# A transformer layer with sixteen heads and top-2 experts: values projected by token rows, moved between partitions and scaled on GpSimd

## The reference

```python
z = _layernorm(patches, ln1_g, ln1_b); z = einsum('bnp,pe->bne', z, W_proj) + b_proj; z = _layernorm(z, ln2_g, ln2_b)
h = concatenate([cls, z]) + pos_emb; h = concatenate([h, txt], axis=1)          # (32, 69, 256)
q, k, v = (einsum('bsd,hpd->bhsp', _layernorm(h), w) + b for each of q, k, v)
attn = softmax(einsum('bhqp,bhkp->bhqk', q, k) / 8, axis=2)                       # over the queries
h = h + einsum('bhqk,bhkp->bqhp', attn, v).reshape(..., 1024) @ l_w.T + l_b
h = h + moe(_layernorm(h))        # top 2 of 8 experts, capacity 690, 256 -> 1024 -> gelu -> 256
```

## Time and profile before

| what | value |
|---|---|
| median of 3 runs | 701.25 us (701.14 to 701.62) |
| the profiled execution: its time, and the span of its profile | 702.5 us, 700.7 us |
| TensorE busy | 682.9 us, 97% |
| VectorE busy | 505.5 us, 72% |
| ScalarE busy | 294.9 us, 42% |
| GpSimd busy | 277.6 us, 40% |
| share of TensorE in the chain that ended last | 73%, VectorE 14% |

### The profile page before, as it was taken

The page is one execution under the profiler, slowest core; times in us unless marked ns, Lnnn a source line. Parts: engine busy times, 40 slices in busy tenths (PEclk is TensorE's granted clock), DMA queues, the critical chain, the costliest instruction groups (busy, mean ns, idle before and its releaser), DMA issues.

```text
span 700.7 us, 16956 instructions
## 1 busy us (share of the span) xinstructions
PE 682.9 (97%) x6671; PEld 649.4 (93%) x6671; DVE 505.5 (72%) x1159; ACT 294.9 (42%) x652; POOL 277.6 (40%) x294
## 2 busy tenths in 40 slices
PE   8999999999999999999999989999999999999995
PEld 6878899999999999999999988999999999999995
DVE  6978876988979889798877756765656484737471
ACT  4454545445454454544544215343424251615130
POOL 4664010130401304011030452766666666665715
PEclk9999999999999999999999999999999999999998
DMA  7931000000000000000000413445454444434203
GB/s 257 271 95 29 2 1 18 12 16 11 19 17 11 17 11 19 18 10 17 12 19 18 138 43 91 121 83 137 69 133 85 112 89 101 103 84 102 24 8 30
DMA packets 51579, 42.99 MB, mean 61 GB/s; under 512 B 25493, under 2 KB 45139, under 8 KB 51515
## 3 DMA queue, kind: packets, MB, share of 16 engines
q1 hardware_dynamic: 20171, 27.85, 12.8%
q0 software_dynamic: 29168, 11.61, 10.5%
q10 hardware_dynamic: 2176, 2.64, 1.3%
HBM read 32.76 MB, written 10.25 MB: 61 GB/s over the span
## 4 chain that ended last, share of the span: by engine, by line
PE 73%; DVE 14%; issue 4%; DMA 3%; SPq 2%; POOL 2%; ACT 1%; POOLq 0%; DVEq 0%; ACTq 0%
PE pair L1518 11%; PE pair L1520 11%; PE pair L1519 11%; PE lone L1518 9%; PE lone L1519 8%; PE lone L1520 8%; PE pair L1636 4%; PE ct_ps L1646 4%; PE vt_ps L1623 3%; DVE vals L1126 2%; DVE zsum L1116 2%; DVE top L1107 2%; SPq L437 2%; DMA raw<-w_qkv 1%; DVE expo L1110 1%
## 5 line engine op out<-in xcount | busy, mean ns | idle before, releaser
L781 POOL DMA_INDIRECT out<-yrow,held x48 | 100.9, 2101 | 62.8 <-DVE yrow L1479 46.3
L1002 ACT ACTIVATE act_f<-pair 128x348 f32<-128x348 f32 (+1 forms) x120 | 49.0, 457 | 92.0 <-PE pair L1520 88.9
L762 POOL DMA_INDIRECT held<-token_rows,found_ix x48 | 70.3, 1464 | 33.5 <-issue 22.0
L1518 PE MATMUL pair<-xe_hi,fc_hi 128*128 128x348 f32 (+1 forms) x256 | 82.1, 321 | 0.6 <-DVE xe_lo L1449 0.3
L1520 PE MATMUL pair<-xe_hi,fc_lo 128*128 128x348 f32 (+1 forms) x256 | 82.2, 321 | 0.0
L1519 PE MATMUL pair<-xe_lo,fc_hi 128*128 128x348 f32 (+1 forms) x256 | 82.1, 321 | 0.0
L1518 PE MATMUL lone<-pj_hi,act_hi 128*116 128x256 f32 (+1 forms) x256 | 72.2, 282 | 0.0
L1520 PE MATMUL lone<-pj_hi,act_lo 128*116 128x256 f32 (+1 forms) x256 | 71.9, 281 | 0.0
L1519 PE MATMUL lone<-pj_lo,act_hi 128*116 128x256 f32 (+1 forms) x256 | 71.8, 280 | 0.0
L845 ACT ACTIVATE expo<-expo 69x552 f32<-69x552 f32 x64 | 42.5, 664 | 55.5 <-DVE expo L1110 54.8
L831 ACT ACTIVATE qkv<-lone,bq_sb 128x276 f32<-128x276 f32 x95 | 46.1, 486 | 36.5 <-PE lone L1520 36.3
(11 more groups left out here) (255 smaller groups left out, 2022.3 us busy)
## 6 DMA issues: line engine op xcount, KB each, us to landing
raw_fc<-c_fc SPq DMA_DIRECT2D x8, 1024.0 KB, 7.0
raw_pj<-c_proj SPq DMA_DIRECT2D x8, 1024.0 KB
raw<-w_qkv SPq DMA_DIRECT2D x6, 512.0 KB, 10.2
out<-h SPq DMA_DIRECT2D x8, 276.0 KB
token_rows<-sent POOLq DMA_DIRECT2D x7, 285.7 KB, 7.0
raw<-patches SPq DMA_DIRECT2D x3, 384.0 KB, 4.9
raw<-patches ACTq DMA_DIRECT2D x3, 384.0 KB, 6.8
raw<-w_l ACTq DMA_DIRECT2D x1, 1024.0 KB, 7.8
```

The costliest lines, as they stand in the source:

```text
L762: pool.indirect_dma_start(xg[p][0:n, t, :], None, x2_dram, bass.IndirectOffsetOnAxis(ap=found_ix[p][0:n, t:t + 1].bitcast(U32), axis=0), b ...
L781: pool.indirect_dma_start(out, bass.IndirectOffsetOnAxis(ap=xg[p][0:n, t, D:D + 1].bitcast(U32), axis=0), yrow[p][0:n, t, :], None, bounds ...
L1002: gelu = act.activation(act_f[f % 2][:, a:b], pair[f % 2][:, h, 0:b - a], ACT.Gelu)
L1518: pe.matmul(dst, l_hi, r_hi, start=(first and n == 0), stop=False)
```

## The change

Values are no longer projected with channels on partitions. A value tile has 92 token rows on partitions and 512 channels (half of the heads) as columns: `project_values` makes six tiles for a group, n = 6g to 6g+5, the first three for units 0 to 3 and the next three for units 4 to 7. It is again `three` for two halves of the depth, so six matmuls of 512 columns. VectorE takes the tile out with its bias (`put_values`) into one of two buffers `value_tile`; SP moves its rows, two DMAs for a tile, so that the rows of each image lie on partitions 0 to 68 (`move_values`, `value_rows`); GpSimd multiplies the 69x512 piece of a unit by the reciprocal sum in two halves (`weigh_values`), except for the last unit, where VectorE does. The value transposes and the third block of a unit are gone; `vt_ps` joins the shared banks as a fifth. The weights are stored so that pieces 0 and 4 hold the values. The buffers lie in the room of the raw weights, so the first use waits for the low parts to be made.

Cut to its core:

```diff
+VALUE_PIECES = (0, 4)
+PAIR_PIECES = (1, 2, 3, 5)
...
-BANKS = 4
+BANKS = 5
...
                 sp.wait_ge(s_h2, g + 1)
                 sp.dma_start(out_tile[:, g * TPG:(g + 1) * TPG, :], h2[:, :, :]).then_inc(s_h2_out, 16)
 
-            for g in range(GROUPS - 1):
-                store_h(g)
+            def move_values(n):
+
+
+                g, k = divmod(n, VTILES)
+                h, t = divmod(k, TPG)
+                if g >= 1 and t == 0:
+                    sp.wait_ge(s_val, UNITS * (g - 1) + (h + 1) * UNITS // 2)
+                if n == TPG:
+                    sp.wait_ge(s_wq_lo, 6)
+                    sp.wait_ge(s_wq_lo2, 6)
+                bank, nth = USE[("value", n, 0)]
+                sp.wait_ge(s_free[bank], nth)
+                for b, n0, r, _, m in VALUE_RUNS[t]:
+                    sp.dma_start(value_rows[h][n0:n0 + m, b // 2, b % 2, :], value_tile[n % 2][r:r + m, :])\
+                        .then_inc(s_moved[n % 2], 16)
+
+            for n in range(TPG):
+                move_values(n)
+            for g in range(GROUPS):
+                if g >= 1:
+                    store_h(g - 1)
+                for n in range(VTILES * g + TPG, min(VTILES * (g + 1) + TPG, VTILES * GROUPS)):
+                    move_values(n)
...
+
+            def weigh_values(m):
+
+                g, u = divmod(m, UNITS)
+                h, n = divmod(u, UNITS // 2)
+                if n == 0:
+                    for p in range(2):
+                        pool.wait_ge(s_moved[p], landed(VTILES * g + (h + 1) * TPG, p))
+                pool.wait_ge(s_zi, m + 1)
+                if m >= 2:
+                    pool.wait_ge(s_ctx, m - 1)
+                v = value_rows[h][:, :, :, n * 128:(n + 1) * 128]
+                for k in range(2):
+                    done = pool.tensor_tensor(
+                        vals[u % 2][:, 4 * k:4 * k + 4, :].rearrange("s (b e) d -> s b e d", e=2),
+                        v[:, k, :, :].rearrange("s b (e d) -> s b e d", e=2),
+                        zinv[u % 2][:, :].rearrange("s (e k b) -> s k b e", e=2, k=2)[:, k, :, :].unsqueeze(3)
+                        .broadcast_to([SEQ, 2, 2, HD]), ALU.mult)
+                done.then_inc(s_val, 1)
...
             def stage_b(g):
-                if g >= 2:
-                    spread(Step(g), -2)
-                if g + 1 < GROUPS:
-                    root_in(Step(g), 1)
+                st = Step(g)
+                more, before = g + 1 < GROUPS, g >= 1
+                weigh_values(UNITS * g)
+                if more:
+                    root_in(st, 1)
                 if g == 0:
                     low_wq(5)
+                if g >= 2:
+                    spread(st, -2)
+                weigh_values(UNITS * g + 1)
+                weigh_values(UNITS * g + 2)
+                if before:
+                    root_mid(st, -1)
+                weigh_values(UNITS * g + 3)
+                if g == 0:
                     rows_here(PT - 1)
                 if g + 2 < GROUPS:
-                    add_positions(Step(g), 2)
+                    add_positions(st, 2)
                 if g == 0:
                     pool.wait_ge(s_masks, 13)
                     pool.wait_ge(s_parts, 16)
-                if g >= 1:
-                    root_mid(Step(g), -1)
-                    weigh(Step(g), -1)
-                    store_x2(Step(g), -1)
+                weigh_values(UNITS * g + 4)
+                weigh_values(UNITS * g + 5)
+                weigh_values(UNITS * g + 6)
+                if before:
+                    widen(st, -1)
+                if more:
+                    weigh_values(UNITS * g + 7)
+                if before:
...
+
+            def put_values(n):
+
+
+                g, k = divmod(n, VTILES)
+                h = k // TPG
+                bank, nth = USE[("value", n, 0)]
+                dve.wait_ge(s_full[bank], nth)
+                if n >= 2:
+                    dve.wait_ge(s_moved[n % 2], landed(n - 1, n % 2))
+                dve.tensor_tensor(value_tile[n % 2], shared[bank][0:TR, 0:VCOLS], bv_sb[:, h * VCOLS:(h + 1) * VCOLS], ALU.add)\
+                    .then_inc(s_free[bank], 1)
 
...
 
+            dve.wait_ge(s_const, 64)
+            dve.wait_ge(s_wq_lo, 3)
+            put_values(0)
             take_max(Step(0), 0)
+            put_values(1)
 
             def unit(m):
...
                     low_ctx(Step((m - 1) // UNITS), (m - 1) % UNITS)
-                weigh_values(st, u)
                 if m + 1 < ALL:
                     take_max(Step((m + 1) // UNITS), (m + 1) % UNITS)
+                n = VTILES * g
+                for i in {2: [3], 3: [5], 6: [6], 7: [8]}.get(u, []):
+                    if n + i < VTILES * GROUPS:
...
+                if m == 0:
+                    put_values(2)
+                if u == 2:
+                    put_values(n + 4)
                 if u == 5 and before:
                     put_logits(st, -1)
                     pick(st, -1, 0)
+                if u == 6 and more:
+                    put_values(n + 7)
                 if u == (6 if more else 5) and before:
                     pick(st, -1, 1)
                 if u == 7 and before and not more:
...
-                done.then_inc(s_vt, 1)
+            def project_values(n):
+
+
+                g, k = divmod(n, VTILES)
+                h, t = divmod(k, TPG)
+                bank, nth = USE[("value", n, 0)]
+                if nth > 1:
+                    pe.wait_ge(s_free[bank], nth - 1)
+                if k == 0:
+                    pe.wait_ge(s_xT_lo, KD * (g + 1))
+                if g == 0 and t == 0:
+                    pe.wait_ge(s_wq_lo, VALUE_PIECES[h] + 1)
+                    pe.wait_ge(s_wq_lo2, VALUE_PIECES[h] + 1)
+                r, w = slice(t * TR, (t + 1) * TR), value_columns(h)
+                x_hi, x_lo = xT_hi[g % 2], xT_lo[g % 2]
+                three(shared[bank][0:TR, 0:VCOLS], [(x_hi[:, k, r], x_lo[:, k, r], wq_hi[:, k, w], wq_lo[:, k, w])
+                                                    for k in range(KD)]).then_inc(s_full[bank], 1)
 
...
+                if m:
+                    score(0)
+                for j in range(2):
                     project_qkv(m, j)
-                    if (m, j) == (1, 0):
-                        score(0)
-            pe.wait_ge(s_const, 48)
+                project_values(m)
+            pe.wait_ge(s_const, 64)
             pe.wait_ge(s_masks, 5)
...
+                for n in value_tiles(m):
+                    project_values(n)
                 if u == (7 if more else 6) and before:
```

More of the change, by code:

```diff
@@ L119, with pair_columns, value_columns, landed @@
 TEXT_RUNS = runs(1 + NPATCH, NTXT)
+VALUE_RUNS = [[run for run in runs(0, SEQ) if run[3] == t] for t in range(TPG)]
+def pair_columns(u, j):
+    at = PAIR_PIECES[u // 2] * PIECE + (2 * (u % 2) + j) * 128
+    return slice(at, at + 128)
+def value_columns(h):
+    return slice(VALUE_PIECES[h] * PIECE, (VALUE_PIECES[h] + 1) * PIECE)
+def landed(n, p):
+    return 16 * sum(len(VALUE_RUNS[i % TPG]) for i in range(p, n, 2))
 class Step:
```

116 lines of the change are left out of this document (69 added, 47 removed).

## The result

The changed kernel takes **867.51 us** (median of 4 runs, 862.18 to 868.23); the kernel before, beside it, 701.37. The ratio is 1.2345 (95% interval 1.2327 to 1.2364). The forecast was 706.0 us, range 697 to 716: slower was right, the size was wrong by 161.5 us.

What follows compares the result with a forecast made beforehand. TensorE was taken as the bound, busy 43.49 of 43.80 us in a group. First group +14.6, six later groups -6.4, last -3.5 gave +4.7 us: 707.2 profiled, 706.0 us as the median, range 697 to 716.

Steps and rivals of the forecast that it cites:

- the landing time: Value moves on SP, issue to landing: 2.2 us taken, from 1.8 for a first load and 3.0 for a row move.
- Tile 3's moves: Later group: they stand behind the residual rows' store on SP, landing at about +8 us from context(1), before tile 5's eviction.
- units 5 to 1: Rest of a later group: products ready 0.1 to 0.6 us ahead, so these units take 28.1 us, before 29.28.
- SP's queue at the start: First group: value moves wait behind all row moves, first issued at 65.05 us; context(0) at 73.5 in place of 59.27.
- TensorE's balance: TensorE per group: loses 10.32 us of transposes and blocks, gains 8.5 of value tiles at 0.236 a matmul: -1.8 us.
- rival (e): Value tiles run below their column price or transposes were dearer; units 5 to 1 save 2.5 us more: 690 us; chance 0.03.
- The later group of 42.8 us: Units 2 to 4 lose their saving to the eviction, move and product chain; group 42.8 us, -1.07, six groups -6.4.
- rival (a): Later groups: TensorE stays the bound as tiles land before context wants them; group 41.6 us, total 697.6; chance 0.17.
- Rival (c): GpSimd's product slowed by collisions with VectorE, 0.37 us each, four a group: +10.6, 716.6 us; chance 0.11.
- Rival (d): TensorE's clock falls in the new pauses, 1.7 us each time; if in every group, +12, 718 us; chance 0.13.
- The sum: Whole kernel: +14.6 first group, -6.4 six later groups, -3.5 last group: +4.7 us, 707.2 for the profiled execution.

Runs made afterwards that it cites:

- the wide run: The change with 69, 46 and 23 rows padded to 80, 48 and 32, or cut into 32 and 14, 16 and 7: 733.27 us.
- the run without moves: The change with all row moves of the values left out, so the products read raw weights: 699.25 us.
- the repaired kernels: The run with both reorderings plus earlier sixth-tile eviction and tile 2's moves ahead of patch 7's rows: 704.01 us; then tile 2 projected earlier, first-half moves before patch 6: 701.17.
- the first four orders tried for SP's queue: The wide run 733.27 us; with value moves between patch row moves 730.27; with moves ahead of a split store of h 722.16; with both 726.86.
- run with both reorderings: The wide run plus first-half value moves between patch row moves, and each group's first value moves ahead of a split store of h: 726.86 us.

## Why the prediction was wrong, and where it was right

**The step that failed** is the landing time, "the moves are 46 to 138 KB, so I take 2.2, nearer the former" (bounds 1.8 and 3.0). It was read from a load of 128 partitions and from row moves of other row counts, as if a transfer's size in KB were all that mattered. For tile 0 it was some 6 us, and for tile 5 of a later group 7.1 us from the eviction to the product instead of 3.0. What mattered was how many DMA engines 69, 46 and 23 rows go over, and that all six moves of a half share the first of them: 138 rows of 0.08 to 0.09 us. The bound from above (3.0) was no bound, as neither row had that property. With the row counts repaired the term was nearly right: in the wide run tile 2's second move was issued at 68.59, the product started 2.5 us later (71.11), and context(0) came at 72.45, 73.5 forecast.

Two statements fell with it. Tile 3's moves "land at about +8, before tile 5 needs its buffer": the eviction of tile 5 waited 4.08 us for them, until +14.1. "In them the products are ready 0.1 to 0.6 us ahead" (units 5 to 1): the product for the next context(0) came 6.29 us late on GpSimd, and these units took 38.5 us instead of 28.1.

**SP's queue at the start** was right: the first value move at 63.48, forecast 65.05, behind all row moves. With wide moves, its order and that of tile 2's projection were worth 8.6 us at context(0) (72.45 to 63.83) of the 14.2 forecast for it.

**TensorE's balance** was right: matmuls of 512 columns follow each other after 0.23 to 0.24 us, here at clock 1.00.

```profile
305.95 0.40 PE L1652 MATMUL lone<-wq_hi,xT_hi 128*92 128x512 f32 x1
306.18 0.40 PE L1653 MATMUL lone<-wq_lo,xT_hi 128*92 128x512 f32 x1
306.42 0.39 PE L1654 MATMUL lone<-wq_hi,xT_lo 128*92 128x512 f32 x1
```

A group's busy time fell from 43.49 us to 42.01 in the run without moves, -1.5 where -1.8 was forecast. The Trainium skill's 131 ns (TensorE: Matmul & The Clock Gate, Back-to-back issue gap) is not seen; rival (e), built on a lower price, is out.

**The later group of 42.8 us** is 42.9 in the repaired kernels and in the run without moves, but for another reason: I had VectorE's chain and the landing set it, with TensorE through in 41.6. With no landing at all it is still 42.9, 42.0 of them busy and about 0.9 in waits for VectorE in units 2 and 3. So **rival (a)**, 41.6 us a group and 697.6 in all, was too low: even with no moves the kernel takes 699.25.

**Rival (c)**, a slow product, is out: halves took 0.62 us, less than the 0.75 taken. **Rival (d)**, the clock, was the right mechanism, too small and not the main one: in the change it fell behind both waits of every group and took 45 of the 169.6 us with it, 5 to 6 us in a group where I had 1.7. Once the moves are short it is worth up to 3.1 us in a group.

**The sum.** 707.2 was forecast for the profiled execution, 867.54 was measured. Up to context(7) of the first group +14.6 us were forecast; it came at 123.34 instead of 92.25, +31.1. From there to the last context(7) (563.10, before 398.01) -9.9 were forecast, and it was +134.0. So most of the miss is the landing term, met twice in every later group, where the sum let one landing eat up a saving, and the clock behind each of these waits. The change's design with landings near 2 us took 722 to 733 us in the first four orders tried for SP's queue, and 704 when two pauses of one to four us were taken out. So the forecast was that of a kernel with other row counts and a better order, and its range didn't reach to what had been read as one number from two unlike rows.

## What to carry to other kernels

Before a transfer goes on the chain, look at the number of rows (partitions) in it, not only at its KB: give it a count with a large divisor up to 16, pad into unused partitions where that is free, and never leave a prime. In a profile, look at the DMA share in short windows during the wait: if it stands in steps of a sixteenth (0.06, 0.13, 0.19), one, two or three engines do it all. And where TensorE is 98% busy, a pause of a microsecond or two in each group can cost more than its own length, so a repair is judged by the granted clock in the groups after it as well.

## What the runs showed of the hardware

- The divisor's weight: 69 rows cut into 67 and 2 cost 120 us over the kernel; 80 rows in place of 69, with 23 and 46 padded or cut as above, take 134 us off. A row of 2 KB takes an engine 0.08 to 0.09 us.
- Moves of a half take 12.5 us at 44 GB/s on the change's counts; with wide ones the DMA engines reach 106 GB/s in the first 6 us.
- TensorE's clock can be held near full by spare matmuls (0.83 to 0.95 in a group). Here they gave back 3.0 us behind context(4) and stood 3.3 us in its way, so that nothing was gained.
- A pause of 1.52 us in an engine that is otherwise busy was followed by 8.5 us at clock 0.60, in which work that takes 5.4 us at 1.00 took 8.47 (run with both reorderings); after one of 1.03 us in the group before (268.93), and after one of 1.47 us in the wide run (230.39), the clock did not fall.
- GpSimd's product of 69x256 with a broadcast operand takes 0.62 us, less than the 0.758 of its plain 128x256 add.
